# One unrolled stage for the two-of-sixteen mixture, with its weight rows spread by DMA, and a spiking layer in nine spans whose spikes TensorE counts

## The reference

```
scores = softmax(xf @ Wg.T)                  # 16 experts
wk, idx = top_k(scores, 2)
cw = sum(one_hot(idx, 16) * wk[..., None], axis=1)
u, g = split(einsum('td,edh->teh', xf, W1))  # 64 + 64 wide for each expert
z = einsum('te,teh,ehd->td', cw, u * silu(g), W2)
ys = gated_mlp(xf @ Ws1) @ Ws2               # shared expert, 128 wide
x = x + z + ys

h = square(relu(x @ W_fc.T)); y = h @ W_proj.T      # 512 wide
repeat 5 times:  reset = mem > 1;  mem = 0.9 * mem + y - reset;  spk = mem > 1
x = x + sum(spk) / 5
```

## Time and profile before

| what | value |
|---|---|
| median of the timed runs | 3194.35 us |
| the profiled execution: its own time / its span | 3164.65 us / 3163.0 us |
| mean granted TensorE clock over the span | 0.917 |
| busy share: TensorE / VectorE / ScalarE / GpSimd | 83% / 75% / 60% / 46% |
| f2r, first TensorE instruction, to the last add of f2 | 2613.05 to 2873.06 us of the span |
| f3, first TensorE instruction, to its last add | 3058.37 to 3151.28 us |

### The profile page before, as it was taken

One profiled execution on the slowest core, in us unless ns is written; L12 is line 12 of the kernel. 1 busy time (PEld: TensorE's weight loads), 2 busy tenths in 40 slices (PEclk: granted clock), 3 DMA queues, 4 the chain that ended last, 5 costly groups with the idle time before them and its releaser, 6 DMA issues. The chain is left out here.

```text
span 3163.0 us, 43653 instructions
## 1 busy us (share of the span) xinstructions
PE 2625.5 (83%) x15621; PEld 968.3 (31%) x15621; DVE 2361.1 (75%) x2857; ACT 1894.3 (60%) x3264; POOL 1453.6 (46%) x2030
## 2 busy tenths in 40 slices
PE   7799999996588589999999429678777786998776
PEld 3122222222256322222222218223222332333222
DVE  6899999985255499999997622679999975446578
ACT  3599999994132379999999105655555541115443
POOL 4666666640654466666662047047777740000000
PEclk9699999998888789999999659879999998999898
DMA  4111111116233301111111321200000000000000
GB/s 123 45 26 28 27 29 26 29 36 119 49 94 101 110 19 26 27 30 27 26 29 40 95 70 35 88 28 21 7 7 14 7 1 0 0 0 12 0 1 27
DMA packets 160320, 117.14 MB, mean 37 GB/s; under 512 B 65301, under 2 KB 138901, under 8 KB 159856
## 3 DMA queue, kind: packets, MB, share of 16 engines
q1 hardware_dynamic: 123312, 75.29, 9.4%
q0 software_dynamic: 36800, 39.15, 4.6%
HBM read 64.26 MB, written 45.67 MB: 35 GB/s over the span
## 5 line engine op out<-in xcount | busy, mean ns | idle before, releaser
L774 DVE TENSOR_REDUCE a_att_mx<-a_att_s 128x2 f32<-128x1024 f32 x960 | 1119.2, 1218 | 90.1 <-PE a_att_s L649 87.9
L753 ACT ACTIVATE a_att_pt<-a_att_st 128x512 f32<-128x512 f32 x2048 | 1085.1, 604 | 74.2 <-PE a_att_st L678 58.8
L678 PE MATMUL a_att_st<-a_qst,a_kst 50*128 50x512 bf16 x2048 | 650.5, 386 | 5.4 <-ACT a_att_pt L753 2.0
L649 PE MATMUL a_att_s<-a_kst,a_qst 48*128 48x512 bf16 x2048 | 585.3, 396 | 61.5 <-PEq L312 32.0
L665 PE MATMUL a_att_av<-a_att_pt,a_att_vst 128*32 128x256 f32 (+1 forms) x7168 | 629.4, 423 | 8.4
L2341 POOL TENSOR_TENSOR g_xn<-m2s_hs,m2s_cb 128x1024 f32<-128x1024 f32 x128 | 300.9, 2357 | 119.0 <-DVE m2s_hs L2308 65.5
L678 PEld LDWEIGHTS a_att_st<-a_qst,a_kst 50*128 50x128 bf16 x2048 | 152.4, 94 | 547.3 <-ACT a_att_pt L753 455.7
L2308 DVE TENSOR_TENSOR_SCAN m2s_hs<-m2s_da,m2s_bps 128x1024 f32<-128x1024 f32 x128 | 292.7, 2287 | 4.4
L530 POOL TENSOR_TENSOR g_area<-g_area 128x512 f32<-128x512 f32 (+3 forms) x256 | 177.8, 695 | 144.2 <-ACT g_area L744 129.1
L665 PEld LDWEIGHTS a_att_av<-a_att_pt,a_att_vst 128*32 128x32 f32 x7168 | 143.3, 108 | 328.7 <-ACT a_att_pt L753 199.2
L2224 PE MATMUL m2s_yps<-g_xn,g_ident 128*128 128x512 f32 x512 | 243.0, 597 | 0.9
(11 more groups left out here) (474 smaller groups left out, 3883.1 us busy)
## 6 DMA issues: line engine op xcount, KB each, us to landing
a_qst<-a_qstk POOLq DMA_DIRECT2D x124, 64.0 KB, 2.3
a_kst<-a_kstk POOLq DMA_DIRECT2D x124, 64.0 KB, 2.4
f_xs<-f_sent SPq DMA_DIRECT2D x20, 396.0 KB, 3.9
a_qstk<-a_qkv_part SPq DMA_DIRECT2D x16, 384.0 KB, 3.4
f_sent<-f0r_zero SPq DMA_DIRECT2D x1, 5148.0 KB, 21.6
a_kstk<-a_qkv_part SPq DMA_DIRECT2D x32, 128.0 KB
a_kstk<-a_qkv_part SPq DMA_DIRECT2D x16, 256.0 KB
g_xn<-a_att_oev SPq DMA_DIRECT2D x256, 16.0 KB
```

What stands on the lines that cost most here:

```text
L649: mm = pe.matmul(s1[:, cut % 2, h, :], qst[u][64 * h:64 * h + SPECIAL, qt * P:(qt + 1) * P], kst[u][64 * h:64 * h + SPECIAL, kh * CH:(kh + ...
L678: pe.matmul(st[:, e % 3, :], kst[u][64 * h:64 * h + STACK, kt * P:(kt + 1) * P], qst[u][64 * h:64 * h + STACK, half * CH:(half + 1) * CH], ...
L753: act.activation(pt[:, e % 16, :], st[:, e % 3, :], ACT.Exp, scale=scale).then_inc(exp_done, 1)
L774: dve.tensor_reduce(mx[:, par, 2 * cut:2 * cut + 2], s1[:, cut % 2, :, :], AX.X, ALU.max).then_inc(s1_used, 1)
```

## The change

The two mixture stages become one, `mixture_stage`, without loops. The shared expert's gate and up products of all 8 chunks (`hold`) are computed while the routing runs, and kept in SBUF; ScalarE changes its function table between silu and exp for that. The token weights are not split and not spread by TensorE: they are turned in float32, copied to SBUF, written to DRAM (8 DMAs), and come back as `share`, one row per expert, spread over 64 partitions by one DMA of 128 KB each (128 DMAs, on SP's queue, in a ring of six). `widen(j)` makes the gate and up products of pair j, `narrow(j - 3)` the down product three pairs behind, and the shared expert's down product opens each chunk. The `sel` weights and their load are gone.

The spiking layer works on nine spans, the first and last of 256 columns, and seven of 512. VectorE no longer counts: it writes each step's spikes as bf16, and TensorE sums the five with an identity matrix in PSUM (`count`), from where the add to x reads them.

```diff
+    def multiply(self, pe, g, between=lambda: None):
...
+        between()
-def turn_parts(pe, parts, ident_b, tps, rows, split_done, steps, copied, turned_sem):
...
-def top2_stage(nc, g, name, w, combT, e, over_all):
...
+def mixture_stage(nc, g, name, route, w):
...
+        def send(engine, half, j):
+            engine.dma_start(by_group[j, :, 4 * half:4 * half + 4, :],
+                             turned[32 * j:32 * j + E, half, :].rearrange("r (c p) -> r c p", p=P)).then_inc(sent[half], 16)
...
+            @block.sync
+            def _(sp):
+                sp.wait_ge(turn_copied[0], 1)
+                send(sp, 0, 0)
+                send(sp, 0, 1)
+                sp.wait_ge(turn_copied[1], 1)
+                for j in range(4):
+                    send(sp, 1, j)
+                for j in range(units):
+                    c, t = j // 8, j % 8
+                    if t == 0:
+                        sp.wait_ge(sent[c // 4], 64)
+                    if j >= 6:
+                        sp.wait_ge(h_done, j - 5)
+                    for i in range(2):
+                        sp.dma_start(share[64 * i:64 * i + 64, j % 6, :], in_dram[2 * t + i:2 * t + i + 1, cols(c)].to_broadcast([64, CH])
+                                     ).then_inc(share_in[j % 6], 16)
...
+                def hold(c):
+                    if c >= 2:
+                        pe.wait_ge(held_done, 2 * (c - 1))
+                    pe.matmul(gp[:, c % 2, :], wg[:, 8, :], g.xn[:, cols(c)], start=True, stop=True)
+                    pe.matmul(up[:, c % 2, :], wu[:, 8, :], g.xn[:, cols(c)], start=True, stop=True).then_inc(held_ready, 1)
+                def widen(j):
+                    c, t = j // 8, j % 8
+                    if j >= 2:
+                        pe.wait_ge(silu_done, j - 1)
+                    else:
+                        pe.wait_ge(held_done, 2 * NCH)
+                    pe.matmul(gp[:, j % 2, :], wg[:, t, :], g.xn[:, cols(c)], start=True, stop=True).then_inc(g_ready, 1)
+                    if j >= 2:
+                        pe.wait_ge(h1_done, j - 1)
+                    pe.matmul(up[:, j % 2, :], wu[:, t, :], g.xn[:, cols(c)], start=True, stop=True).then_inc(u_ready, 1)
+                def narrow(j):
+                    c, t = j // 8, j % 8
+                    if t == 0:
+                        if c >= 2:
+                            pe.wait_ge(y_added, c - 1)
+                        pe.wait_ge(shared_done, c + 1)
+                        pe.matmul(yp[:, c % 2, :], wd[:, 8, :], shared[:, c % 2, :], start=True, stop=False)
+                    pe.wait_ge(h_done, j + 1)
+                    mm = pe.matmul(yp[:, c % 2, :], wd[:, t, :], h[:, j % 4, :], start=False, stop=t == 7)
+                    if t == 7:
+                        mm.then_inc(y_ready, 1)
+                pe.wait_ge(w.here, w.all)
+                found.multiply(pe, g, lambda: hold(0))
+                for c in range(1, NCH):
+                    hold(c)
+                pe.wait_ge(comb_ready, 1)
+                pe.wait_ge(comb_zero, 1)
+                for half in range(2):
+                    for c in range(4):
+                        for j in range(4):
+                            mm = pe.matmul(tps[32 * j:32 * j + 32, half, c * P:(c + 1) * P],
+                                           comb[:, 4 * (4 * half + c) + j, :], g.ident[:, :], start=True, stop=True)
+                    mm.then_inc(turn_done, 1)
+                for j in range(units):
+                    widen(j)
+                    if j >= 3:
+                        narrow(j - 3)
+                for j in range(units - 3, units):
+                    narrow(j)
...
+                def first(j):
+                    c = j // 8
+                    if j % 8 == 0:
+                        dve.wait_ge(held_done, 2 * c + 2)
+                        if c >= 2:
+                            dve.wait_ge(y_ready, c - 1)
+                        dve.tensor_tensor(shared[:, c % 2, :], held_g[:, c, :], held_u[:, c, :], ALU.mult).then_inc(shared_done, 1)
+                    dve.wait_ge(silu_done, j + 1)
+                    dve.wait_ge(u_ready, j + 1)
+                    dve.tensor_tensor(h1[:, j % 5, :], sg[:, j % 2, :], up[:, j % 2, :], ALU.mult).then_inc(h1_done, 1)
+                def second(j):
+                    c = j // 8
+                    if j % 8 == 4 and c >= 1:
+                        add_y(c - 1)
+                    dve.wait_ge(h1_done, j + 1)
+                    dve.wait_ge(share_in[j % 6], 32 * (j // 6 + 1))
+                    dve.tensor_tensor(h[:, j % 4, :], h1[:, j % 5, :], share[:, j % 6, :], ALU.mult).then_inc(h_done, 1)
...
+                dve.tensor_tensor(comb[:, :, 0:E], oh1[:, :, :], oh2[:, :, :], ALU.add).then_inc(comb_ready, 1)
+                dve.wait_ge(turn_done, 2)
+                dve.tensor_copy(turned[:, 1, :], tps[:, 1, :]).then_inc(turn_copied[1], 1)
+                for j in range(units):
+                    first(j)
+                    if j >= 2:
+                        second(j - 2)
+                second(units - 2)
+                second(units - 1)
...
+                def hold(c):
+                    act.wait_ge(held_ready, c + 1)
+                    act.activation(held_g[:, c, :], gp[:, c % 2, :], ACT.Silu).then_inc(held_done, 1)
+                    act.copy(held_u[:, c, :], up[:, c % 2, :]).then_inc(held_done, 1)
+                act.preload_act_table_set("silu_and_others")
                 found.copy_rows(act)
+                for c in range(5):
+                    hold(c)
+                act.preload_act_table_set("natural_log_exp_and_others")
+                act.wait_ge(diff_ready, 1)
+                act.activation(w2[:, :], m2[:, :], ACT.Exp).then_inc(exp_ready, 1)
+                act.wait_ge(diff_ready, 2)
+                act.activation(ex[:, :, :], ex[:, :, :], ACT.Exp).then_inc(exp_ready, 1)
                 act.preload_act_table_set("silu_and_others")
-def glu_stage(nc, g, name, tiles, w, combT, rows, ahead):
...
+                for c in range(5, NCH):
+                    hold(c)
+                act.wait_ge(turn_done, 1)
+                act.copy(turned[:, 0, :], tps[:, 0, :]).then_inc(turn_copied[0], 1)
+                act.wait_ge(turn_copied[0], 1)
+                send(act, 0, 2)
+                send(act, 0, 3)
...
 def spike_stage(nc, g, name, w):
+    edges = [0] + [CH // 2 + c * CH for c in range(NCH)] + [TOK]
+    spans = [slice(lo, hi) for lo, hi in zip(edges, edges[1:])]
...
+        spikes = s.sb("spikes", [P, 2, steps, CH], BF16)
+        zp, yp, cp = s.ps("zp", [P, 3, CH]), s.ps("yp", [P, 2, CH]), s.ps("cp", [P, 2, CH])
...
+                def count(c):
+                    pe.wait_ge(spiked, c + 1)
+                    if c >= 2:
+                        pe.wait_ge(added, c - 1)
+                    for t in range(steps):
+                        mm = pe.matmul(cp[:, c % 2, 0:wide[c]], g.ident_b[:, :], spikes[:, c % 2, t, 0:wide[c]],
+                                       start=t == 0, stop=t == steps - 1)
+                    mm.then_inc(counted, 1)
...
+                for j, (c, t) in enumerate(units):
+                    if j >= 3:
+                        pe.wait_ge(relu_done, j - 2)
+                    pe.matmul(zp[:, j % 3, 0:wide[c]], wfc[:, t, :], g.xn[:, spans[c]], start=True, stop=True).then_inc(z_ready, 1)
+                    if j >= 1:
+                        down(j - 1)
+                    if t == tiles - 1 and c >= 2:
+                        count(c - 2)
+                down(len(units) - 1)
+                count(n_spans - 2)
+                count(n_spans - 1)
...
+                    if t == tiles - 1:
+                        if c >= 3:
+                            act.wait_ge(spiked, c - 2)
+                        act.wait_ge(y_ready, c + 1)
+                        act.copy(y[:, c % 3, 0:wide[c]], yp[:, c % 2, 0:wide[c]]).then_inc(y_copied, 1)
...
+                def add(c):
+                    x = g.xT[:, spans[c]]
+                    dve.wait_ge(counted, c + 1)
+                    dve.scalar_tensor_tensor(out=x, in0=cp[:, c % 2, 0:wide[c]], scalar=1.0 / steps, in1=x, op0=ALU.mult,
+                                             op1=ALU.add).then_inc(added, 1)
...
+                for c in range(n_spans):
+                    at = slice(0, wide[c])
+                    now = y[:, c % 3, at]
+                    dve.wait_ge(y_copied, c + 1)
+                    if c >= 2:
+                        dve.wait_ge(counted, c - 1)
+                    last = now
+                    dve.tensor_scalar(spikes[:, c % 2, 0, at], last, 1.0, None, ALU.is_gt)
+                    for t in range(1, steps):
+                        if t > 1:
+                            dve.wait_ge(stepped, per * c + 2 * (t - 1))
+                        dve.scalar_tensor_tensor(out=u_[:, c % 2, at], in0=last, scalar=0.9, in1=now,
```

(17 more changed lines are left out.)

238 lines of the change are left out of this document (67 added, 171 removed).

## The result

| | before | after |
|---|---|---|
| median, first occasion | 3193.64 us (3192.1 to 3198.84) | 3117.4 us (3114.17 to 3128.67) |
| ratio, with its 95% interval | | 0.9767 (0.9752 to 0.9782) |
| profiled execution, its own time / span | 3164.65 / 3163.0 us | 3117.75 / 3116.0 us |
| mixture, first gate row to last add | 260.0 us | 197.3 us |
| between it and the spiking layer | 185.3 us | 182.8 us |

The changed kernel is faster by 76 us, 2.3%. The forecast was 3129 (range 3112 to 3148). By the traces 62.7 us come from the mixture (forecast 59), 8.5 from the spiking layer (forecast 6), and 2.5 from the layer between them with its norms, whose code is the same in both (forecast nothing). Together that is 73.7; the other 2.5 of the 76 stand in no trace.

What follows compares the result with a forecast made beforehand. TensorE bounds the mixture, VectorE's dependent chain the routing and VectorE the spiking layer. Savings of 59 us in the mixture and 6 in the spiking layer, 65 together, taken from the median 3194.35 give 3129 us, range 3112 to 3148.

Steps and rivals of the forecast that it cites:

- rival B: Mixture start and spiking layer: TensorE keeps ahead, counting hides in ScalarE's stall, start-up quick; 74 us less, 3120; chance 0.12.
- Steady part: Mixture: 72 turns of 3.09 us become 200 products of 0.857, a turn of 2.57; 51.1 us less.
- Rival A: Exposed waits cost 0.1 us per mixture pair, start-up slow, spiking layer gains only 2; 48 less, 3146; chance 0.12.
- The weight load: Mixture's 51-row spreading product: its load is not pulled ahead, leaving 0.3 us exposed at its two borders.
- The start: Mixture before its pair products: first gate product at 2639.5 instead of 2642.54, on the clock of before.
- The first held pair: Mixture start: standing between gate rows and turning to tokens, it delays the VectorE chain by 3.0 us.
- the turning: Mixture start: 64 TensorE passes with 32-column weights, taken at 3.4 us between bounds of 2.1 and 7.2.
- The stall of 1.5 for the first `h`: Mixture start: TensorE waits 1.5 us because the first share rows land 3.4 to 5.5 after issue.
- The tables: Routing: ScalarE's table load of 1.28 us is just hidden; at 2.66 per switch the saving would be about 56.
- The spiking layer: TensorE and ScalarE's loop becomes the bound at 9.3 us per span, over VectorE's 8.3; 6 us less.
- Rival C: Mixture: share rows arrive one pair after another, a landing of 4.8 us per pair; slower, 3269; chance 0.04.
- Rival D: Mixture: held products delay the routing by more than they save, say 15 us; 50 less, 3144; chance 0.06.

Runs made afterwards that it cites:

- e2: Only the changed mixture stage, with the spiking layer of the kernel before: 3099.15 us, ratio 0.9803 to before.
- e4: Kernel before with selection weights and turned token weights zero-padded from 51 to 128 rows: 3147.22 us, ratio 0.9951 to before.
- e7: Changed kernel with the shared expert's held products made after the turning of the token weights: 3103.75 us, ratio 0.981 to before.
- e10: Changed kernel with eight spans of 512 in the spiking layer instead of nine, TensorE counting: 3091.91 us, ratio 0.9772 to before.
- e6: Changed kernel with a span's counting products moved behind the next span's second hidden product, where TensorE waits: 3087.91 us, ratio 0.975 to before.
- e8: Changed kernel with each pair's two share DMAs issued only after the previous pair's landed: 3165.65 us, ratio 1.0004 to before.
- e11: Changed kernel with every share-row DMA issued twice, the second into a spare ring nothing reads: 3120.46 us, ratio 0.9863 to before.
- e1: Kernel before, unchanged, run again on the second occasion: 3161.69 us, ratio 0.9999 to before.
- e5: Changed kernel, unchanged, run again on the second occasion: 3090.52 us, ratio 0.9765 to before.

## Why the prediction was right

The likeliest case came about in its mechanism: TensorE is the bound of the mixture, the spread costs it nothing, and in the spiking layer the loop of TensorE and ScalarE takes VectorE's place. The size was 11 us short, and that the result still lies in the range is in part luck, since the range was widened for the rivals. Its own terms allowed 3121 to 3138, and 3117.4 lies outside them, nearer to rival B (3120) than to the forecast (3129). Half of B came true, the quick start; the other half, counting that hides in ScalarE's stall, did not. The 11 us are 3.7 in the mixture, 2.5 in the spiking layer, 2.5 in the layer between, which the prediction put at nothing without saying so, and 2.5 between traces and medians.

- Steady part. Forecast 0.857 per product and a turn of 2.57; measured 0.86 and 2.58. From the first pair product to the end of the last add it is 173.5 us, forecast 174.4 (171.4 + 1.5 + 0.6 + 0.85). e2 shows it alone. Rival A, 0.1 in each pair, is out.
- The weight load. The 0.3 us that the prediction put at the borders of the 51-row product are shown by e4, which takes them away. The rule that it drew on does not explain them. The Trainium skill (TensorE: Matmul & The Clock Gate, Step-by-step: what each phase is for) names two cases in which a load is pulled ahead of a running product: its row groups do not conflict with it, or it goes to the background weight buffer. The first does not tell 51 rows from 128, since both share row groups with a running 128-row product, and yet e4's 128-row load starts 0.43 ahead; the second says nothing of rows. So it does not follow from the rule that 128-row weights have no exposed load, but it is what the traces show: the counting group takes 1.07, without the 0.2 that the sum gave it.
- The start was the mis-sized term of the mixture: 26.5 forecast, 23.8 measured. The first held pair cost 2.0 of delay, not 3.0; the turning 1.96, not 3.4. The 3.4 was a middle value between rows 6 and 7, both at a granted clock of 1.00, and the measured 1.96 lies just under the lower bound of 2.1 worked out from them. That e7, where TensorE had idled, measures 3.43 is coincidence: the prediction had not asked at which clock the turning would run.
- The stall of 1.5 for the first `h` did not come. SP's six sends took 2.70 us in all, near the forecast, but a row of 128 KB lands 3.0 after its issue and not after the 3.4 to 5.5 of the 256 KB ones; the first, issued at 2666.22, was in place by 2669.86.
- The tables. The load was just hidden, as forecast (a wait of 0.23). The Trainium skill's 2.66 us per switch (ScalarE: Activation LUTs, What ACT_TABLE_LOAD costs) does not show: next functions start 0.01 to 0.02 us after loads of 1.28 end.
- The spiking layer. 9.3 per span was right (9.31), but in part by luck: the terms add up to 9.4, rounded down, and hold 0.2 too much for the counting. y of the second span came 15.3 us after the first product, forecast 15.2. VectorE's own span is 7.6 (first comparisons at 3090.11 and 3097.70, nothing waited for) where 8.3 was forecast, which shows only in the last one and a half spans, together with a first period of 8.7. Forecast 6, measured 8.5. The half span at the head does bring the first comparison 3.1 forward, as worked out (7.2 us after the first product, 10.3 with the eight spans of e10), and keeps it until the eighth span (70.1 against 73.4). But then nine spans have a half one left, and it takes the 3.1 back: 14.2 us to the last add against 10.8. Rival B's "counting hides" is what e6 does.
- Rival C was named and priced from landings of 4.8; made on purpose (e8) the mean turn is 3.7 and the kernel ends level with before, close to the 3.6 at which the prediction put the turning point. Rival D: e7 shows that the held products delay the turning by 2.7 us and save 13.9 in all.
- The spreading DMAs were costed at nothing, which holds at 98 GB/s and two issues per turn. e11 shows how near the limit is: four issues at 0.64 fill a turn of 2.57.
- The 30 us between median and profiled execution were taken as the kernel's own and lasting. They are not (e1, e5); the difference was unharmed because both kernels were timed on one occasion.

## What to carry to other kernels

Look at how many rows a stationary operand (the weights) has: here one with 51 rows between full ones cost more at its borders (0.30 us) than its product did (0.22), and zero rows cured it. A stage that fills TensorE's idle time also raises its clock for what follows (1.96 us instead of 3.43 for the same 64 passes), so ask of every duration that you take over at which clock it was measured and at which it will run. Where a new group of products goes is worth as much as its size: put it where the engine already waits (e6). When a transfer comes late, look at the queue that issues it before you blame the transfers (e11).

## What was not expected of the hardware

- Spreading rows of 2 KB over 64 partitions occupies the DMA engines to 86 to 100% at 175 to 178 GB/s (e11), where the 256 KB ones moved 256 GB/s; with twice the traffic a row lands 6.2 us after issue instead of 3.0, and an issue by SP takes 0.69 us in the mean, where the changed kernel's take 0.45 and 0.60 in turn.
- Identical code lost 30 us beside GpSimd's scatters on one occasion and nothing on another; a profile can come from the other level than the timed runs.
- The 183 us behind the mixture depend on it: 182.8 in the changed kernel (e5 too), 187.1 after e8 and e11, 185.3 after before. In the first 20 us of it the granted clock is 0.90, 0.83, 0.83 and 0.79, which is not the order of the times, so the clock alone does not carry it. What does was not tried.
